# Attention inside a hybrid block on one core: single-bank score tiles in a ring of three, values left with channels on partitions, row sums inverted on a small tile, q and k stored in halves

## The chip, the cores and the metric

The kernel runs on one core of a Trainium2 chip, as one program. The time is device microseconds from the first to the last instruction of the program, and smaller is better. The names of the engines are those of the profile: PE is TensorE (PEld its weight loads), ACT ScalarE, DVE VectorE, POOL GpSimd, SP SyncE.

## The reference, cut to what matters

Four layers follow each other on x of shape 16 x 1024 x 256: windowed attention, a mixture of experts, full attention, and the mixture of experts again, each on a layer norm of x and added to x. The change touches the third.

```python
def _L0_attn_b_ref(x, w_qkv, w_o):
    b, s, hid = x.shape                      # 16, 1024, 256
    heads, d = 16, hid // 16                 # 16 heads of 16 channels
    qkv = x @ w_qkv.T * hid ** (-0.5)
    qkv = qkv.reshape(b, s, 3, heads, d)
    q, k, v = (jnp.transpose(qkv[:, :, i], (0, 2, 1, 3)) for i in range(3))
    scores = jnp.einsum('bhqd,bhkd->bhqk', q, k) * d ** (-0.5)
    attn = jax.nn.softmax(scores, axis=-1) * (s / np.sqrt(s - 1.0))
    out = jnp.einsum('bhqk,bhkd->bhqd', attn, v) * s ** (-0.5)
    out = jnp.transpose(out, (0, 2, 1, 3)).reshape(b, s, hid)
    return out @ w_o.T * hid ** (-0.5)
...
x = x + _L0_attn_b_ref(_layernorm(x, axis=-1), L0_attn_b_w_qkv, L0_attn_b_w_o)
```

## The kernel before, in words

`projection_stage` (names with cp_) makes q, k and v for 32 groups of 512 tokens and stores them to DRAM. q and k are stored twice, as a rounded part ("hi") and the rest ("lo"), so that products can be taken in the fast float32r form.

`attention_stage` (names with at_) works on 128 **pairs**: two heads of one batch, 8 pairs to a batch, 16 batches. The loop over pairs is unrolled. Every engine has its own written list of instructions, and semaphores join them.

For one pair, the scores are computed twice.

- **Scores by query** (`scores_by_query`, L1830): 16 steps (8 tiles of 128 queries by 2 halves of the keys), each two matmuls of 128x512, one for each head, into one of the two buffers psM (two banks each). DVE takes the maximum over each (`maximum`, L1773, 128x1024 elements). They run 5 query tiles more than one pair ahead (`LEAD`). After 16 of them `mx` (L1777) joins the halves, PE turns it (`max_rows`, L1836), ACT negates it (`take_max`, L1721), POOL splits it into hi and lo (`split_max`), and SP writes the two as rows 48 and 49 of the queries' tile (`load_max`, L1618 and L1619). The matmul then subtracts the maximum by itself.
- **Scores by key** (`scores_by_key`, L1846): 32 tiles of 128 keys by 512 queries. psE has three banks. The tiles are taken in 21 groups of 2, 1, 2, 1, ... tiles (`GROUPS`): the twos use banks 0 and 1, the ones bank 2. A group's matmul waits for the exponential of the group two before (`p_ready`), and ACT takes the exponential of a whole group in one instruction (`exps`, L1729), of 1024 or 512 elements a partition.
- **Values** (`values`, L1857): for each of 8 key tiles, 8 matmuls of 256 queries, in four column groups of the array, gather probabilities times (v, 1) into the one bank psO, with 16 channels and the row sum on partitions. A pair's last two key tiles are done in the next pair.

The result of a pair: ACT copies psO to OT (`take_values`, L1734), PE turns it back into psO with four transposes (`turn_values`, L1867), DVE takes the reciprocal of the sums and multiplies (`normalise`, L1784 and L1788) into O. Four pairs later PE turns pieces of O (`turn_out`, L1873), ACT copies them (`take_out`, L1739), POOL splits them (`split_out`, L1683 and L1686), and `project_out` (L90 with at_w) makes one unit of 128 tokens of the output in bank 2. ACT scales it (`scale_y`, L1744), POOL adds x (`add_x`, L1693), and SP stores it (L1630) and loads the next x (L1622).

The order on PE is written out by hand in `pair`: each `key(g)`, `query(m, g)` and `values(...)` stands at a fixed place. PE, DVE and ACT take their lists strictly in turn, and so does SP, which per pair waits for the pair before to be through with its tiles, issues 9 loads of q, k and v for the pair three ahead, then 4 for the maxima, one store and one load.

Of the kernel before, what the change touches and what calls it, by code (L numbers as in the profile page):

```python
# [1275 lines left out]
def projection_stage(nc, T, stage, x, wT, qk, v):  # L1276
# [5 lines left out]
    G = 512  # L1282
# [3 lines left out]
    qkb = qk.rearrange("r (b h) d n -> b r (h d) n", h=H)  # L1286
    vb = v.rearrange("b p s h k w -> s b p h k w")
    with ExitStack() as ctx:
# [34 lines left out]
        def _(sp):  # L1323
# [156 lines left out]
def attention_stage(nc, T, stage, x, qk, v, woT, out):  # L1480
# [10 lines left out]
    NG = 21  # L1491
    OUT_SCALE = S / float(S - 1) ** 0.5 * S ** -0.5 * D ** -0.5
    xb = x.rearrange("(b p q c) d -> b c q p d", q=4, c=2, p=128)
    ob = out.rearrange("(b q c p) d -> b c q p d", q=4, c=2, p=128)
    qkp = qk.rearrange("r (u x) d n -> u x r d n", x=2)
    vp = v.rearrange("b p s (u x) k w -> u b p s (x k w)", x=2)
    with ExitStack() as ctx:
# [11 lines left out]
        rden = sb("rden", [128, 2, KC], F32)  # L1509
        O = sb("o", [128, KC, D], F32)  # L1510
# [23 lines left out]
        oT_ready, t_done, o_ready, rden_ready = sem("oT_ready"), sem("t_done"), sem("o_ready"), sem("rden_ready")  # L1534
        xo_done, xo_taken, xo_hi_ready, xo_lo_ready = sem("xo_done"), sem("xo_taken"), sem("xo_hi_ready"), sem("xo_lo_ready")
# [7 lines left out]
        GROUPS = [(3 * g // 2, 2) if g % 2 == 0 else ((3 * g + 1) // 2, 1) for g in range(NG)]  # L1543
        HOLDS = [next(g for g in range(NG) if GROUPS[g][0] + GROUPS[g][1] > u) for u in range(4 * KC)]
        LEAD = 5
        OUT_AT, MAX_AT, VALUES_AT, NORM_AT = 1, 11, 3, 3
# [39 lines left out]
        def load_queries(eng, pp, j):  # L1586

            for a in range(2):
                r = 64 * a
                eng.dma_start(Q[j][r:r + 32, :].bitcast(F32), row(qkp, pp)[a, 0:2]).then_inc(qk_loaded[j], 16)  # L1590
                eng.dma_start(Q[j][r + 32:r + 48, :].bitcast(F32), row(qkp, pp)[a, 0]).then_inc(qk_loaded[j], 16)

        def load_keys(eng, pp, j):

            for a in range(2):
# [3 lines left out]
                eng.dma_start(K[j][r:r + 16, :].bitcast(F32), row(qkp, pp)[a, 2]).then_inc(qk_loaded[j], 16)  # L1599
                eng.dma_start(K[j][r + 16:r + 48, :].bitcast(F32), row(qkp, pp)[a, 2:4]).then_inc(qk_loaded[j], 16)  # L1600
# [6 lines left out]
        def _(sp):  # L1607
# [13 lines left out]
            def load_x(b, n):  # L1621
                sp.dma_start(X[n][:], row(xb, b)[n // 4, n % 4]).then_inc(x_loaded[n], 16)  # L1622

            def store_out(u, b, n):
# [29 lines left out]
            batches(pair)
            store_out(NP - 9, B - 2, PB - 1)
            for n in range(PB):
                store_out(PB * B - PB + n, B - 1, n)
            for n in range(PB):
                sp.wait_ge(y_stored[n], 16 * B)

        @block.gpsimd
        def _(pool):
# [343 lines left out]
```

## Time and profile before

| | before |
|---|---|
| median of 3 runs | 5755.92 us (5751.49 to 5757.47) |
| the profiled execution's own time | 5750.62 us |
| its span | 5748.9 us |
| granted TensorE clock, mean | 0.976 |
| PE, PEld busy | 94%, 64% |
| DVE, ACT, POOL busy | 78%, 62%, 26% |

The attention stage is slices 15 to 33 of the page's 40 (about 2005 to 4799 us), nearly half of the kernel. PE's busy time is modelled: matmuls overlap in the array, so PE can stand at 100% and still have waited. What PE waited for is seen at its weight loads (PEld), since each matmul's load carries the wait. In the list of DMA issues the columns are KB each and us from issue to landing. In the timeline a row is a run of like instructions: start, duration, engine, line, count, and in brackets the idle time ahead and who ended it.

### The profile page before, as it was taken

The page shows a single profiled execution, that of the slowest core. Times are in us where ns is not written, and L with a number is a line of the kernel's source. Part 1 is how long each engine was busy: PE and PEld are TensorE (multiplying, and loading weights), DVE is VectorE, ACT ScalarE, POOL GpSimd, SP SyncE. Part 2 cuts the span into 40 slices and gives each one's busy share as a digit, 9 for nine tenths or more (in the row PEclk, how much of TensorE's full clock was granted, in tenths as well). Part 3 has the DMA queues.
Part 4 walks back from the last instruction along what each step waited for, and adds up shares of the span by engine and source line. Part 5 has one row for each costly group of instructions (what it writes and reads, how often), then busy time and mean ns, then how long its engine had stood idle before and what let it go on. Part 6 is the DMA issues. An engine that isn't in the chain of part 4 may idle for free. (4 is left out here: it accounts for less than half of the span.)

```text
span 5748.9 us, 131254 instructions
## 1 busy us (share of the span) xinstructions
PE 5428.0 (94%) x50092; PEld 3660.4 (64%) x50092; DVE 4498.2 (78%) x7377; ACT 3566.0 (62%) x5406; POOL 1473.5 (26%) x1948
## 2 busy tenths in 40 slices
PE   7999668999989889999999999999999997799999
PEld 6777457999978734444444444444444444699998
DVE  7888695555557689999999999999999996755554
ACT  5777562333325458888888888888888886433332
POOL 4655453333310000111111111111111114533332
PEclk9999889999999989999999999999999998999999
DMA  2222482222229811121112111111211113222221
GB/s 74 78 84 78 137 259 77 88 93 93 89 96 333 310 56 49 58 60 57 57 59 60 57 56 60 59 57 56 60 58 57 57 54 104 75 89 93 95 86 49
DMA packets 317697, 512.58 MB, mean 89 GB/s; under 512 B 36442, under 2 KB 221156, under 8 KB 311152
## 3 DMA queue, kind: packets, MB, share of 16 engines
q1 hardware_dynamic: 291912, 441.44, 24.2%
q0 software_dynamic: 24576, 64.56, 3.5%
q8 instruction: 271, 4.44, 0.3%
q10 hardware_dynamic: 808, 1.07, 0.1%
q14 instruction: 130, 1.06, 0.1%
HBM read 338.59 MB, written 185.60 MB: 91 GB/s over the span
## 5 line engine op out<-in xcount | busy, mean ns | idle before, releaser
L1773 DVE TENSOR_REDUCE at_best<-at_psM 128x2 f32<-128x1024 f32 x2048 | 2430.7, 1221 | 227.5 <-PE at_psM L1830 214.3
L1729 ACT ACTIVATE at_p<-at_psE 128x1024 f32<-128x1024 f32 (+1 forms) x2688 | 2077.1, 824 | 529.5 <-PE at_psE L1846 515.7
L1846 PE MATMUL at_psE<-at_q,at_k 50*128 50x512 f32 x4096 | 1174.0, 436 | 7.5 <-ACT at_p L1729 6.3
L1830 PE MATMUL at_psM<-at_k,at_q 48*128 48x512 f32 x4096 | 1093.6, 458 | 37.5 <-DMA at_k<-scratch_qk 27.4
L1857 PE MATMUL at_psO<-at_p,at_v 128*17 128x256 f32 x16384 | 1109.9, 383 | 0.1
L1122 ACT ACTIVATE e_h_hi<-e_psH 128x512 fp32r<-128x512 f32 x512 | 306.7, 599 | 916.0 <-PE e_psH L90 864.4
L1846 PEld LDWEIGHTS at_psE<-at_q,at_k 50*128 50x128 f32 x4096 | 548.7, 185 | 462.4 <-issue 223.6
L1196 DVE SCALAR_TENSOR_TENSOR e_h_lo<-e_psH,e_h_hi 128x512 fp32r<-128x512 f32 x512 | 353.9, 691 | 595.9 <-ACT e_h_hi L1122 505.8
L1857 PEld LDWEIGHTS at_psO<-at_p,at_v 128*17 128x17 f32 x16384 | 364.1, 96 | 542.7 <-issue 345.4
L1830 PEld LDWEIGHTS at_psM<-at_k,at_q 48*128 48x128 f32 x4096 | 471.3, 185 | 312.2 <-DVE at_best L1773 147.2
L90 PE MATMUL e_psE<-e_w_hi,e_h_hi 128*128 128x256 f32 x2048 | 583.1, 285 | 0.0
L90 PE MATMUL e_psE<-e_w_hi,e_h_lo 128*128 128x256 f32 x2048 | 579.6, 283 | 0.0
L90 PE MATMUL e_psE<-e_w_lo,e_h_hi 128*128 128x256 f32 x2048 | 579.3, 283 | 0.0
L90 PE MATMUL e_psH<-e_xhi,e_w_hi 128*128 128x512 f32 x1024 | 406.8, 397 | 4.7 <-DVE e_xlo L1163 4.7
L90 PE MATMUL e_psH<-e_xlo,e_w_hi 128*128 128x512 f32 x1024 | 406.1, 397 | 0.0
L90 PEld LDWEIGHTS e_psE<-e_w_hi,e_h_hi 128*128 128x128 f32 x2048 | 391.3, 191 | 21.6 <-issue 1.2
L90 PEld LDWEIGHTS e_psE<-e_w_lo,e_h_hi 128*128 128x128 f32 x2048 | 391.4, 191 | 17.3
L90 PE MATMUL e_psH<-e_xhi,e_w_lo 128*128 128x512 f32 x1024 | 400.0, 391 | 0.0
L90 PEld LDWEIGHTS e_psE<-e_w_hi,e_h_lo 128*128 128x128 f32 x2048 | 391.1, 191 | 0.0
L1672 POOL CAST at_nm_hi<-at_nm 16x128 fp32r<-16x128 f32 x128 | 36.0, 282 | 1258.3 <-ACT at_nm L1721 1258.3
L1693 POOL TENSOR_TENSOR at_y<-at_y,at_x 128x256 f32<-128x256 f32 x120 | 87.5, 729 | 1029.9 <-ACT at_y L1744 1029.9
L258 POOL COPY a_pt<-a_pc 32x512 f32<-32x512 f32 x384 | 236.1, 615 | 114.7 <-PE a_psO L541 32.7
(213 smaller groups left out, 8456.5 us busy)
## 6 DMA issues: line engine op xcount, KB each, us to landing
e_w_raw<-in_w SPq DMA_DIRECT2D x64, 1024.0 KB
scratch_qk<-cp_qkh SPq DMA_DIRECT2D x64, 512.0 KB
scratch_qk<-cp_qkl SPq DMA_DIRECT2D x64, 512.0 KB
at_q<-scratch_qk SPq DMA_DIRECT2D x256, 128.0 KB
at_k<-scratch_qk SPq DMA_DIRECT2D x252, 128.0 KB
scratch_v<-cp_va SPq DMA_DIRECT2D x32, 544.0 KB
at_v<-scratch_v SPq DMA_DIRECT2D x126, 136.0 KB, 10.0
a_x<-in_x SPq DMA_DIRECT2D x32, 512.0 KB
```

The lines of the kernel that those rows point to most:

```text
L90: last = nc.tensor.matmul(out, a, b, start=start and n == 0, stop=stop and n == len(products) - 1, **kw)
L258: nc.gpsimd.tensor_copy(PT[b][r, :, r], PC[b][r, :, :]).then_inc(pt_ready, 1)
L1122: nc.scalar.activation(h_hi[f % 2][:], psH[f % 2][:, 0:G], ACT.Relu).then_inc(h_hi_ready, 1)
L1196: nc.vector.scalar_tensor_tensor(out=h_lo[f % 2][:], in0=psH[f % 2][:, 0:G], scalar=0.0, in1=h_hi[f % 2][:].bitcast(F32), op0=ALU.max, op1 ...
L1672: nc.gpsimd.tensor_copy(nm_hi[s][:], nm[s][:]).then_inc(nm_hi_ready, 1)
L1693: nc.gpsimd.tensor_tensor(Y[n][:], Y[n][:], X[n][:], ALU.add).then_inc(y_ready, 1)
L1729: nc.scalar.activation(P[:, u:u + n, :], src, ACT.Exp, scale=HD ** -0.5).then_inc(p_ready, 1)
L1773: nc.vector.reduce_max(best[j % 2][:, h, :, qt], psM[h][:], AX_X).then_inc(m_taken, 1)
L1830: last = nc.tensor.matmul(psM[h][:, a, :], Q[j][r, 128 * qt:128 * qt + 128], K[j][r, 512 * h:512 * h + 512], start=True, stop=True)
L1846: last = nc.tensor.matmul(psE[:, u - u0 if n == 2 else 2, :], K[j][r, 128 * kc:128 * kc + 128], Q[j][r, 512 * half:512 * half + 512], star ...
L1857: last = nc.tensor.matmul(psO[32 * q:32 * q + HD + 1, 256 * a:256 * a + 256], V[j][:, kc // 4, a, kc % 4, :], P[:, 4 * kc + 2 * (q // 2) + ...
```

## The change

1. **Score ring.** `GROUPS` goes. Each of the 32 tiles is a unit of its own with its own exponential of 512 elements; psE is a ring of three banks in which the tiles, `max_rows` (before tile 14) and `project_out` (before tile 19) take turns (`IN_TURN`, `bank`, `wait_for_bank`). A tile's matmul waits for the user of its bank three turns before. PE's list in `pair` is written anew, and the values of a pair lag more: key tiles 3 to 7 are done in the next pair.
2. **Values stay with channels on partitions.** `turn_values`, `normalise`, `turn_out` and `take_out` go. SP stores OT to DRAM (`store_values`) and moves the sums, SBUF to SBUF, onto a tile of 128x16 (`sums`). DVE inverts that (`invert`, after its maximum 11 of 16). SP stores it (`store_inverses`), and four pairs later loads values and inverses back, the latter repeated over 16 channels (`load_unit`). POOL multiplies (`split_out`). The end of the stage has tiles of its own (`divide_end`).
3. **q and k in halves.** The DRAM tensor is split by half of the sequence, so `projection_stage` stores contiguous blocks, and `load_queries` and `load_keys` issue 12 loads of 16 rows by 2 by 512 in place of 8, four of which had 32 rows.
4. **Order elsewhere.** SP's and POOL's lists are rearranged; tokens of x and of the output are taken in plain tiles of 128 strided by 8.

```diff
-    NG = 21
+    NU, BANKS = 4 * KC, 3
-        OUT_AT, MAX_AT, VALUES_AT, NORM_AT = 1, 11, 3, 3
+        OUT_AT, MAX_AT, VALUES_AT, INVERT_AT = 19, 14, 14, 11
+        IN_TURN = [user for u in range(NU) for user in (["out"] if u == OUT_AT else ["max"] if u == MAX_AT else []) + [u]]
+        def bank(pp, user):
+            return psE[:, turn_at_bank(pp, user) % BANKS, :]
...
+            def store_values(p):
+                sp.wait_ge(oT_ready, p + 1)
+                sp.dma_start(ot[p].rearrange("a r c -> r a c"), OT[:].rearrange("r (a c) -> r a c", a=2)).then_inc(oT_stored, 16)
...
+                    sp.dma_start(sums[p % 2][:], OT[HD:128:32, :].rearrange("q (w e) -> q w e", e=16)).then_inc(sums_moved, 16)
+            def load_unit(u, slot, b, k, m, needed):
...
+                sp.dma_start(raw[slot][:], rows[b, k, m][:, 0:HD, :]).then_inc(unit_loaded[slot], 16)
+                sp.dma_start(den[slot][:], inverse_rows[b, k, m].unsqueeze(1).broadcast_to([8, HD, 256])).then_inc(unit_loaded[slot], 16)
...
             def split_out(u, slot, k, m, b):
-                pool.wait_ge(xo_taken, u + 1)
+                pool.wait_ge(unit_loaded[slot], 32 * (u // 2 + 1))
+                after(pool, xo_lo_ready, u - 1)
+                nc.gpsimd.tensor_tensor(oT[slot][:], raw[slot][:], den[slot][:], ALU.mult).then_inc(ofT_ready, 1)
+                pool.wait_ge(ofT_ready, u + 1)
                 after(pool, wo_done, PB * (b - 1) + 2 * m + 2)
...
+            def exps(pp, u):
+                act.wait_ge(e_done, NU * pp + u + 1)
+                if u % 4 == 0:
+                    after(act, pv_done, KC * (pp - 1) + u // 4 + 1)
+                nc.scalar.activation(P[:, u, :], bank(pp, u), ACT.Exp, scale=HD ** -0.5).then_inc(p_ready, 1)
             def take_values(p):
                 act.wait_ge(pv_done, KC * p + KC)
-                after(act, t_done, p)
+                after(act, oT_stored, 16 * p)
+                after(act, sums_moved, 16 * p)
...
+            def invert(p):
+                dve.wait_ge(sums_moved, 16 * (p + 1))
+                nc.vector.reciprocal(sums[p % 2][:], sums[p % 2][:]).then_inc(rden_ready, 1)
...
+                last_values(3), keys(0), query(0, 1), keys(1), query(1, 2), keys(2), last_values(4, (0,))
+                last_values(4, (1,)), keys(3, 5), query(2, 5), keys(5), last_values(5, (0,))
+                keys(6), query(3, 7), keys(7), last_values(5, (1,)), query(4, 8), keys(8, 11), last_values(6)
+                query(5, 11), keys(11, 13), query(6, 13), keys(13), last_values(7)
+                next_max_rows(), query(7, 14), keys(14, 16), query(8, 16), keys(16), values(pp, pb % 4, 0)
+                keys(17, 19), query(9, 19), output(), keys(19), query(10, 20), keys(20), query(11, 21)
+                keys(21), values(pp, pb % 4, 1, (0,)), keys(22, 24), values(pp, pb % 4, 1, (1,)), query(12, 24), keys(24), query(13, 25)
+                keys(25, 27), values(pp, pb % 4, 2, (0,)), keys(27), query(14, 28), keys(28), values(pp, pb % 4, 2, (1,))
+                keys(29), query(15, 30), keys(30, 32)
```

In the lists at_psE<-at_q,at_k is a score tile by key, at_psM<-at_k,at_q one by query, at_psO<-at_p,at_v the values. PE before, from the output unit of a steady pair to the turned values:

```order
L90 MATMUL at_psE<-at_w_hi,at_oT_lo 128x256
L1830 MATMUL at_psM<-at_k,at_q 128x512 x2
L1846 MATMUL at_psE<-at_q,at_k 128x512 x2
L1857 MATMUL at_psO<-at_p,at_v 17x256 x8
L1830 MATMUL at_psM<-at_k,at_q 128x512 x4
L1846 MATMUL at_psE<-at_q,at_k 128x512 x3
L1857 MATMUL at_psO<-at_p,at_v 17x256 x8
L1846 MATMUL at_psE<-at_q,at_k 128x512
L1830 MATMUL at_psM<-at_k,at_q 128x512 x2
L1846 MATMUL at_psE<-at_q,at_k 128x512 x2
L1867 MATMUL at_psO<-ident,at_oT 128x128 x4
```

PE in the change, from query step 3 of a steady pair to key tile 13:

```order
L1900 MATMUL at_psM<-at_k,at_q 128x512 x2
L1927 MATMUL at_psE<-at_q,at_k 128x512
L1937 MATMUL at_psO<-at_p,at_v 17x256 x4
L1900 MATMUL at_psM<-at_k,at_q 128x512 x2
L1927 MATMUL at_psE<-at_q,at_k 128x512 x3
L1937 MATMUL at_psO<-at_p,at_v 17x256 x8
L1900 MATMUL at_psM<-at_k,at_q 128x512 x2
L1927 MATMUL at_psE<-at_q,at_k 128x512 x2
L1900 MATMUL at_psM<-at_k,at_q 128x512 x2
L1927 MATMUL at_psE<-at_q,at_k 128x512
```

Key tiles now come one by one, three in a row at most, and some value blocks are halved; the transposes of the values are gone from the list.

SP before, from the last loads of k to the end of a steady pair:

```order
L1599 DMA at_k<-scratch_qk 16x1024
L1600 DMA at_k<-scratch_qk 32x1x1024
L1604 DMA at_v<-scratch_v 128x2x136
L1618 DMA at_q<-at_nm_hi 1x8x128
L1619 DMA at_q<-at_nm_lo 1x8x128
L1618 DMA at_q<-at_nm_hi 1x8x128
L1619 DMA at_q<-at_nm_lo 1x8x128
L1630 DMA out_x<-at_y 128x256
L1622 DMA at_x<-scratch_x 128x256
```

SP in the change, from the loads of q and k of a steady pair to its end:

```order
L1608 DMA at_q<-scratch_qk 16x2x512 x6
L1617 DMA at_k<-scratch_qk 16x2x512 x6
L1621 DMA at_v<-scratch_v 128x2x136
L1655 DMA scratch_ot<-at_oT 128x2x256
L1659 DMA at_sums<-at_oT 128x1x16
L1635 DMA at_q<-at_nm_hi 1x8x128
L1636 DMA at_q<-at_nm_lo 1x8x128
L1635 DMA at_q<-at_nm_hi 1x8x128
L1636 DMA at_q<-at_nm_lo 1x8x128
L1665 DMA scratch_rd<-at_sums 4x32x16
L1647 DMA out_x<-at_y 128x256
L1639 DMA at_x<-scratch_x 128x256
```

The value and sum transfers stand ahead of the four for the maxima, the inverses behind them; with the two loads of a unit, which stand in front, SP issues 24 transfers a pair, 15 before.

## Rows read from the trace of the kernel before

**Rows 1.** Windows, steady stretch (stretch, length, busy us by engine, PEclk, DMA share, GB/s).

```profile
3500.00:4000.00 500.00, 500.00 (x4809) 246.15 (x4809) 459.31 (x445) 404.34 (x586) 58.98 (x116) 1.00 0.19 58
```

**Rows 2.** Groups by line and form, 3000 to 4500 us.

```profile
L1773 DVE TENSOR_REDUCE at_best<-at_psM 128x2 f32<-128x1024 f32 x1126 | 1337.7, 1221 | 116.2 <-PE at_psM L1830 108.4
L1729 ACT ACTIVATE at_p<-at_psE 128x1024 f32<-128x1024 f32 x774 | 792.5, 1024 | 96.4 <-PE at_psE L1846 89.2
...
L1729 ACT ACTIVATE at_p<-at_psE 128x512 f32<-128x512 f32 x703 | 424.2, 603 | 188.9 <-PE at_psE L1846 188.9
...
L1686 POOL TENSOR_TENSOR at_oT_lo<-at_ofT,at_oT_hi 128x256 fp32r<-128x256 f32 x70 | 51.2, 731 | 12.6 <-POOL at_oT_hi L1683 12.6
...
L1777 DVE TENSOR_TENSOR at_mx<-at_best 128x16 f32<-128x16 f32 x71 | 12.4, 175 | 2.4
```

**Rows 3.** Waits, 3000 to 4500 us (waiting engine <- releaser: total us, times, longest).

```profile
ACT at_p L1729 <- PE at_psE L1846: 278.0, 632, 0.8
...
DVE at_best L1773 <- PE at_psM L1830: 108.4, 351, 0.5
PEld at_psE L1846 <- ACT at_p L1729: 102.5, 351, 0.4
POOL at_oT_hi L1683 <- PE at_psE L90: 80.6, 9, 9.0
PEld at_psM L1830 <- DVE at_best L1773: 67.7, 212, 0.4
```

**Rows 4.** Timeline of the stage's start, PE clock still at half.

```profile
2024.13 1.22 PE L1830 MATMUL at_psM<-at_k,at_q 48*128 48x512 f32 x4 [27.43 <-DMA at_k<-scratch_qk]
2024.97 18.19 DVE L1773 TENSOR_REDUCE at_best<-at_psM 128x2 f32<-128x1024 f32 x16 [15.31 <-PE at_psM L1830]
2026.25 0.80 PE L1830 MATMUL at_psM<-at_k,at_q 48*128 48x512 f32 x2 [0.90 <-DVE at_best L1773]
...
2051.39 0.64 SPq L1619 DMA_DIRECT2D at_q<-at_nm_lo  x1
...
2054.26 0.66 PE L1846 MATMUL at_psE<-at_q,at_k 50*128 50x512 f32 x2
```

**Rows 5.** Timeline of one steady pair, DVE and ACT.

```profile
4001.25 0.60 ACT L1734 ACTIVATE at_oT<-at_psO 128x512 f32<-128x512 f32 x1
4001.73 3.15 ACT L1729 ACTIVATE at_p<-at_psE 128x512 f32<-128x512 f32 x4
...
4002.88 0.25 DVE L1784 RECIPROCAL at_rden<-at_psO 128x16 f32<-128x16 f32 x1
4003.16 0.42 DVE L1788 TENSOR_TENSOR at_o<-at_psO,at_rden 128x256 f32<-128x256 f32 x1
4003.50 2.35 DVE L1773 TENSOR_REDUCE at_best<-at_psM 128x2 f32<-128x1024 f32 x2
```

**Rows 6.** Timeline of three places in a steady pair, PE, ACT and DVE.

```profile
3500.01 1.06 PE L1857 MATMUL at_psO<-at_p,at_v 128*17 128x256 f32 x16
...
3501.00 0.49 PE L1846 MATMUL at_psE<-at_q,at_k 50*128 50x512 f32 x1
...
3514.16 0.50 PE L1846 MATMUL at_psE<-at_q,at_k 50*128 50x512 f32 x1
...
3514.69 1.51 ACT L1729 ACTIVATE at_p<-at_psE 128x512 f32<-128x512 f32 x2 [0.38 <-PE at_psE L1846]
...
3520.22 0.50 PE L1830 MATMUL at_psM<-at_k,at_q 48*128 48x512 f32 x2
...
3520.76 3.56 DVE L1773 TENSOR_REDUCE at_best<-at_psM 128x2 f32<-128x1024 f32 x3 [0.44 <-PE at_psM L1830]
```

**Rows 7.** SP's issue of one 16-row load; DMA issues of one pair; a window of it.

```profile
3534.16 0.40 SPq L1591 DMA_DIRECT2D at_q<-scratch_qk  x1
...
at_v<-scratch_v SPq DMA_DIRECT2D x1, 136.0 KB, 10.1
...
out_x<-at_y SPq DMA_DIRECT2D x1, 128.0 KB, 4.2
...
3542.00:3543.00 1.00, 1.00 (x15) 0.53 (x15) 0.91 (x1) 0.68 (x2) 0.00 (x0) 1.00 0.14 52
```

**Rows 8.** Timeline of the last two pairs, of which DVE has next to nothing, and of the end.

```profile
4747.78 0.60 ACT L1734 ACTIVATE at_oT<-at_psO 128x512 f32<-128x512 f32 x1
...
4768.49 0.60 ACT L1734 ACTIVATE at_oT<-at_psO 128x512 f32<-128x512 f32 x1
...
4786.26 0.60 ACT L1734 ACTIVATE at_oT<-at_psO 128x512 f32<-128x512 f32 x1 [1.18 <-PE at_psO L1857]
...
4789.39 1.42 DVE L1812 TENSOR_TENSOR at_oT_lo<-at_psM,at_oT_hi 128x256 fp32r<-128x256 f32 x4 [1.07 <-ACT at_oT_hi L1766]
```

**Rows 9.** Windows, projection stage.

```profile
1800.00:1820.00 20.00, 19.92 (x117) 16.46 (x115) 14.39 (x40) 9.67 (x16) 0.00 (x0) 1.00 0.97 334
```

More of the change, by code:

```diff
@@ L1477, in _, with attention_stage @@
             groups(pe, NG, group)
[L1480 removed]
+def attention_stage(nc, T, stage, x, qk, v, ot, rd, woT, out):
     N, D = x.shape
@@ L1654, in _ @@
             batches(pair)
+            store_values(NP - 1)
+            sp.wait_ge(oT_stored, 16 * NP)
+            for m in range(4):
+                span = slice(256 * m, 256 * m + 256)
+                sp.dma_start(end_den[:, span], rows[B - 1, 1, m][:, HD:HD + 1, :].broadcast_to([8, HD, 256])).then_inc(end_loaded[m], 16)
+                sp.dma_start(end_raw[:, span], rows[B - 1, 1, m][:, 0:HD, :]).then_inc(end_loaded[m], 16)
             store_out(NP - 9, B - 2, PB - 1)
@@ L1659, in _ @@
                 sp.wait_ge(y_stored[n], 16 * B)
+            for s in range(2):
+                sp.wait_ge(rden_stored[s], 16 * (NP // 2 - s))
         @block.gpsimd
@@ L1697, in pair @@
             def pair(pp, pb, b):
+                if there(pp + 1):
+                    split_max(pp + 1, (pb + 1) % 4, turn_of(pp, pb, b, -1) + 1 if not first(pp) else 0)
                 if has_out(pp):
@@ L1700, in pair @@
                     add_x(u, ub, n)
-                if there(pp + 1):
-                    split_max(pp + 1, (pb + 1) % 4, turn_of(pp, pb, b, -1) + 1 if not first(pp) else 0)
                 if has_turned(pp):
@@ L1832, in scores_by_query, with wait_for_bank @@
                 last.then_inc(m_done, 1)
-            def max_rows(p, j):
+            def wait_for_bank(pp, user):
+                n = turn_at_bank(pp, user) - BANKS
+                while n >= 0:
+                    pp, before = n // len(IN_TURN), IN_TURN[n % len(IN_TURN)]
+                    if before == "out" and has_out(pp):
+                        return pe.wait_ge(y_scaled, pp - 8)
+                    if before == "max" and there(pp + 1):
+                        return pe.wait_ge(nm_ready, pp + 2)
+                    if before != "out" and before != "max":
+                        return pe.wait_ge(p_ready, NU * pp + before + 1)
+                    n = n - 1
@@ L1900, in query, with keys @@
                         scores_by_query(mp, mj, turn_of(pp, pb, b, 1 if m // 2 < KC - LEAD else 2), qt, m % 2,
[L1901 to L1911 removed]
+                                        u % 2)
+                def keys(u, end=0):
+                    for each in range(u, max(u + 1, end)):
+                        scores_by_key(pp, pb % 4, turn_of(pp, pb, b, 0), each)
                 def last_values(kc, heads=(0, 1)):
@@ L1934, in pair @@
-                output(), query(0, -1), key(0), last_values(6)
-                query(1, 0), query(2, 0), key(1), key(2), last_values(7)
-                key(3), query(3, 3), key(4)
-                if not first(pp):
-                    turn_values(pp - 1)
-                key(5), query(4, 5), query(5, 5), key(6), values(pp, pb % 4, 0)
-                key(7), query(6, 7), key(8), values(pp, pb % 4, 1)
-                key(9), query(7, 9), key(10), query(8, 10), turns(), values(pp, pb % 4, 2, (0,))
@@ L1942, in pair @@
-                query(9, 10), key(11), key(12), values(pp, pb % 4, 2, (1,))
-                values(pp, pb % 4, 3, (0,)), query(10, 12), key(13), query(11, 13), key(14), values(pp, pb % 4, 3, (1,))
-                values(pp, pb % 4, 4, (0,)), key(15), query(12, 15), key(16), values(pp, pb % 4, 4, (1,))
-                key(17), query(13, 17), query(14, 17), key(18), key(19), values(pp, pb % 4, 5)
-                key(20), query(15, 20)
+                        project_out(ub, n, bank(pp, "out"))
```

218 lines of the change are left out of this document (108 added, 110 removed).

## Prediction

> **What bounds the kernel now.** I read the windows of the steady stretch first, then the groups, the waits, and the timeline of single pairs. A pair takes 1500 us / (1126 / 16) = 21.31 us [rows 2], and 128 pairs are nearly the whole stage. In the windows PE is busy all the time, DVE 92%, ACT 81% [rows 1]; none of these is the floor. DVE's floor is in the start of the stage, where nothing but maxima run: 16 in 18.19 us, so (18.19 - 1.22) / 15 = 1.131 us each, 18.1 us a pair [rows 4]. The reciprocal and the product cost it 4003.50 - 4002.88 = 0.62 us [rows 5], `mx` 0.18 [rows 2]: 18.9 us, so DVE stands 2.4 us of each pair. ACT loses more: it waits for score tiles 278.0 us in this stretch, 3.9 us a pair [rows 3]. PE waits for ACT 102.5 us and for DVE 67.7 us at these two tiles alone, 1.5 and 1.0 us a pair [rows 3].
>
> So the three wait for one another. The telling rows are those of the last pair but one: from one copy of the values to the next it takes 4768.49 - 4747.78 = 20.71 us [rows 8], though DVE has almost nothing left to do there. The bound is the loop of PE and ACT through psE. The reason is in its geometry: a group of two tiles can only be refilled when its own exponential is through, and only the one-tile exponential covers that. From the row at 3514.69, 1.51 - 1.02 = 0.49 us is the step of a 512-element exponential with work waiting, and PE's key tile at 3514.16 was 0.53 us ahead of it [rows 6]; 0.53 + 0.05 against 0.49 and the second tile's 0.1 leaves ACT idle before each large group, 0.38 us in that row.
>
> **The change part by part.**
>
> *Ring.* ACT's floor: 32 exponentials at 0.48 (the step from 4001.25 to 4001.73 [rows 5]) are 15.4 us, with the copies of values, maxima and output about 16.3 us. A bank now has two other exponentials, 0.96 us, to be refilled in, against 0.05 + 0.53 = 0.58 us needed, so PE may be 0.4 us late before ACT stands. PE gains freedom, but ACT runs closer to it.
>
> *PE.* Gone are six transposes (0.9 us by the timeline's gaps, an estimate from the 0.5 to 1.0 us pieces of [rows 6]), and the waits for OT and for the group ahead. Added are entries into value blocks: a block of 16 instructions takes 3501.00 - 3500.01 = 0.99 us [rows 6], two halves a little more together. I take PE's work as 17.5 us, below DVE's.
>
> *DVE.* Product and half the cost of the reciprocal go: 18.1 + 0.18 + 0.25 (the reciprocal's own 0.25 [rows 5], its input now in SBUF) = **18.55 us, the new floor**. What comes on top is how late PE brings a query step. A step may start 2026.25 - 2024.97 = 1.28 us after the start of the maximum two before it [rows 4], and the next maximum can start 3520.76 - 3520.22 = 0.54 us after the step [rows 6]; 1.28 + 0.54 = 1.82 against 2 x 1.131 leaves PE 0.44 us of slack. I followed PE's new list with 0.11 us a score tile, 0.99 or 0.56 us a value block or half, 0.9 us for the output unit and these lags. Three places lose time. Tiles 8 to 10 wait for exponentials 5 to 7, the block of key tile 6 follows, and query step 5 comes 0.5 us late. Step 10 behind the output unit is 0.1 late. At the pair's end tiles 29 to 31 and another block stand between steps 15 and 0, 0.4 us. The sum is 18.55 + 1.0 = 19.6 us; I take **19.7 us**, since entries into blocks were left out. The ends are 18.55 us (no gap) and 18.55 + 2.4 = 20.95 us (DVE's gaps stay). The saving is 128 x (21.3 - 19.7) = **205 us**, between 350 and 45.
>
> *SP.* It issues 24 transfers a pair instead of 15. At the 0.64 us of the row at 2051.39 [rows 4] that is 15.4 us of 19.7, with its waits in between. The loads of q and k start at the pair's head, and are through (12 x (0.40 [rows 7] + 0.05) = 5.4 us) before the values of the pair before are done (about 8.5 us in, by the walk above). Hidden, if the pair is no shorter than 16 us; otherwise the issue itself is the floor.
>
> *The trip of the sums.* ACT copies the values after its tile 13, about 9.5 us in. SP issues the store and then the small transfer (by 10.7 us); the nearest small transfer, the last row of the maxima, was issued at 2051.39 and its reader ran at 2054.26, so 2.9 us at most [rows 4]. The sums are there at 13.6 us; DVE wants them after maximum 11, 12 x 1.14 + 1 = 15 us in. Hidden by 1.4 us. The range of landings is 2.9 to 10.1 us, the latter of the values' load [rows 7]; I take the small one, because the 10 us are those of a transfer queued behind slow loads. What queues behind it: every later maximum on DVE, and with it PE's query steps.
>
> *Loads of q and k.* While the 32-row loads ran, the DMA share was 0.14 and 52 GB/s [rows 7], some two engines of 16. The new form has 16 rows. This shortens queueing in every pair, which costs nothing there, and the wait at the stage's start, 27.43 us [rows 4]: I take 6 us off, of 0 to 12. The Trainium skill (DMA: Bandwidth & Descriptors, Rules for kernel authors) says that the outermost dimension of the patterns sets how many engines a transfer gets, and a source of 2 x 16 x 1024 would get two; the trace agrees with its 0.14, and by that rule the gain would be the upper end.
>
> *POOL.* It gets one product more, at the 0.73 us of the row of L1686 [rows 2], in 15 us of slack. But it takes its list in turn, and `split_out` of a batch's last unit waits for that span's output unit of the batch before. It did so 9 times for 9.0 us [rows 3]. The unit now stands 12 us into the next pair instead of at its head, and `split_max` is queued behind. From there: 12.4 + 1.1 for the split + 0.8 for `split_max` + 2.0 for SP + 2.9 to land = 19.2 us, against 19.7 when the next pair's first tile needs it. I take 0.5 us for 15 batches, **8 us**, between 0 and 30.
>
> *End of stage.* The last pair has three more value blocks behind its exponentials (3 us, some of it given back by a first pair that has them not). From the copy at 4786.26 to the first difference at 4789.39 it took 3.1 us [rows 8]; now two transfers to and from DRAM at 4.2 us each [rows 7] and some 1.5 us of DVE and ACT lie there: **9 us** more, between 5 and 12.
>
> *Projection stage.* 32 stores become contiguous. PE is busy 19.92 of 20 us [rows 9], so nothing, between -5 and +3.
>
> Against the profiled execution's own time: 5750.6 - 205 - 6 + 8 + 9 = 5557 us. The median of the runs lies 5.3 us above that execution, so 5562; I say **5560 us**.
>
> **The rivals.**
>
> 1. *The gaps stay.* PE serves two rings from one list, and the ring by key wants service every 0.48 us. DVE's gaps of 2.4 us stay and 0.3 us or more is all that is saved: 20.6 to 21 us a pair, 5650 to 5715 us. For it: PE's slack of 0.44 us is half a value block. Against it: the 20.71 us of a pair without DVE [rows 8] belong to the geometry that goes.
> 2. *The sums come late, and it is slower.* Place: the wait ahead of `invert`. If the transfer lands later than 15 - 10.7 = 4.3 us after its issue, all of the excess stops DVE in every pair. From 4.3 + 1.6 = 5.9 us it eats the gain. At the 10.1 us of the values' load [rows 7] a pair takes 19.7 + 5.8 = 25.5 us, and the kernel 5560 + 128 x 5.8 = 6300 us; at 7 us, 5905. For it: 64-byte pieces, and a queue with 24 transfers. Against it: the slow loads ahead of it go.
> 3. *A fixed cost for each exponential.* ACT has 11 exponentials more a pair. At the whole 603 ns of a single one [rows 2] 32 are 19.3 us, with the copies 20.5 us a pair, 5665 us, already a smaller gain. The Trainium skill (ScalarE: Activation LUTs, Rules for kernel authors) gives about 0.3 us an instruction and 0.83 ns an element, which would be 32 x 0.72 = 23 us, and a kernel some 300 us slower. The trace disagrees: the step is 0.48 to 0.49 us [rows 5, 6].
> 4. *Nothing moves*, because a chain over pairs (maxima, POOL, SP) takes the place: 21.3 us.
>
> **How the numbers follow.** The forecast has 0.72: pairs of 18.9 to 20.5 us, 5450 to 5665 us. Rival 1 has 0.15, all of it faster. Rival 2 has 0.07, rival 3 has 0.02 and rival 4 has 0.04, most of it within the bound. About 0.2%, 12 us, is what a measurement of this kernel can tell from no change. Faster: 0.72 + 0.15 + 0.01 = 0.88; same 0.03; slower 0.07 + 0.02 = 0.09. The range reaches down to 5450 and up to 5680 us, which takes in the lower part of rival 1 and leaves out 0.05 below and 0.15 above.
>
> **What the profile will show.** Maxima every 19.5 to 20 us by sixteen, with DVE at 93 to 95%. ACT's wait for score tiles from 3.9 to about 2 us a pair, its exponentials in long unbroken runs. No wait of DVE on the sums; their landing under 4 us. q and k landed 6 us after the first issue. A longer wait of PE for ACT at single tiles would show rival 1; a wait "DMA at_sums" on DVE, rival 2; ACT near 100% busy, rival 3. I am wrong in the reason if the pair gets shorter while ACT's wait for PE stays.

## The result, and the profile after

| | before | changed |
|---|---|---|
| median | 5756.69 us (5751.49 to 5758.22, 4 runs) | 5680.16 us (5677.24 to 5697.62, 4 runs) |
| ratio, 95% interval | | 0.9875 [0.9854, 0.9896] |
| profiled execution, span | 5750.62, 5748.9 | 5697.62, 5695.9 |
| DVE, ACT, PE busy | 78%, 62%, 94% | 78%, 64%, 94% |

The change is faster, by 76.5 us (1.3%); the forecast was 196 us, and 5680.2 lies just above its range. The direction came true, the size did not.

First the steady stretch again. Windows of the changed kernel, with the columns of [rows 1, 7, 9]:

```profile
3500.00:4000.00 500.00, 497.52 (x4817) 228.03 (x4817) 458.17 (x436) 429.64 (x846) 80.61 (x147) 1.00 0.30 87
1800.00:1820.00 20.00, 19.88 (x118) 16.27 (x116) 14.29 (x38) 9.84 (x18) 0.00 (x0) 1.00 0.96 336
```

DVE is as busy as in [rows 1], 92%, not the 93 to 95% that I named. The second row answers to [rows 9]: the projection stage did not move. Groups and waits of 3000 to 4500 us, as in [rows 2, 3]:

```profile
L1839 DVE TENSOR_REDUCE at_best<-at_psM 128x2 f32<-128x1024 f32 x1160 | 1360.2, 1220 | 124.1 <-PE at_psM L1900 117.9
L1801 ACT ACTIVATE at_p<-at_psE 128x512 f32<-128x512 f32 x2320 | 1214.0, 598 | 207.2 <-PE at_psE L1927 178.0
```

```profile
PEld at_psE L1927 <- ACT at_p L1801: 196.7, 508, 0.4
...
ACT at_p L1801 <- PE at_psE L1927: 178.0, 437, 0.7
POOL at_oT_hi L1757 <- PE at_psE L90: 169.6, 9, 18.8
...
DVE at_best L1839 <- PE at_psM L1900: 117.9, 290, 0.6
```

1160 / 16 = 72.5 pairs in 1500 us are 20.69 us each, 0.6 less than before. From copy to copy of the values the trace gives 20.70 us, the same to 0.07 us in the whole steady stretch. ACT's wait for score tiles fell from 3.9 to 178.0 / 72.5 = 2.5 us a pair, as the ring was meant to do. DVE's did not fall: 117.9 / 72.5 = 1.6 us against 1.5. The timeline of one pair shows where it stands:

```profile
4001.16 1.06 PE L1937 MATMUL at_psO<-at_p,at_v 128*17 128x256 f32 x16
...
4002.14 0.50 PE L1900 MATMUL at_psM<-at_k,at_q 48*128 48x512 f32 x2
...
4002.69 1.23 DVE L1839 TENSOR_REDUCE at_best<-at_psM 128x2 f32<-128x1024 f32 x1 [0.53 <-PE at_psM L1900]
...
4002.96 0.40 PE L1927 MATMUL at_psE<-at_q,at_k 50*128 50x512 f32 x1
...
4003.28 1.06 PE L1937 MATMUL at_psO<-at_p,at_v 128*17 128x256 f32 x16
...
4007.75 1.23 DVE L1839 TENSOR_REDUCE at_best<-at_psM 128x2 f32<-128x1024 f32 x1 [0.22 <-PE at_psM L1900]
...
4009.31 2.36 DVE L1839 TENSOR_REDUCE at_best<-at_psM 128x2 f32<-128x1024 f32 x2 [0.34 <-PE at_psM L1900]
...
4011.59 0.24 DVE L1849 RECIPROCAL at_sums<-at_sums 128x16 f32<-128x16 f32 x1
...
4016.92 5.93 DVE L1839 TENSOR_REDUCE at_best<-at_psM 128x2 f32<-128x1024 f32 x5 [0.53 <-PE at_psM L1900]
...
4023.41 1.23 DVE L1839 TENSOR_REDUCE at_best<-at_psM 128x2 f32<-128x1024 f32 x1 [0.56 <-PE at_psM L1900]
```

DVE stands ahead of step 5 (4002.69), behind the output unit (4009.31) and at the pair's end (4016.92, with the next pair's step 5 again at 4023.41). These are the three places of the prediction, but with larger gaps, and a small fourth stands ahead of step 9 (4007.75). And look at PE's rows: a value block takes 4002.14 - 4001.16 = 0.98 us, as read before, but it starts 4003.28 - 4002.96 = 0.32 us behind the last tile, where tiles follow each other in about 0.12. That is 0.2 us at each entry into a block, which stands in no row by itself.

The ends of the stage. Its start, as in [rows 4], then its end, as in [rows 8]:

```profile
2033.00 1.22 PE L1900 MATMUL at_psM<-at_k,at_q 48*128 48x512 f32 x4 [16.47 <-DMA at_k<-scratch_qk]
```

```profile
4706.51 0.62 ACT L1807 ACTIVATE at_oT<-at_psO 128x512 f32<-128x512 f32 x1
...
4707.72 0.57 SPq L1659 DMA_DIRECT2D at_sums<-at_oT  x1
...
4709.65 0.25 DVE L1849 RECIPROCAL at_sums<-at_sums 128x16 f32<-128x16 f32 x1 [18.80 <-DMA at_sums<-at_oT]
...
4720.47 0.60 ACT L1807 ACTIVATE at_oT<-at_psO 128x512 f32<-128x512 f32 x1 [3.48 <-PE at_psO L1937]
...
4727.22 1.75 DVE L1855 RECIPROCAL at_end_den<-at_end_den 128x256 f32<-128x256 f32 x1 [17.32 <-DMA at_end_raw<-scratch_ot]
...
4732.16 0.42 DVE L1882 TENSOR_TENSOR at_oT_lo<-at_end_raw,at_oT_hi 128x256 fp32r<-128x256 f32 x1
```

PE waited 16.47 us for k, against 27.43: 11.0 us less. At the end 4732.16 - 4720.47 = 11.7 us lie between the last copy of values and the first difference, against 3.1 before, 8.6 more. Landings, as in [rows 7]:

```profile
at_q<-scratch_qk SPq DMA_DIRECT2D x768, 64.0 KB, 2.4
...
at_v<-scratch_v SPq DMA_DIRECT2D x126, 136.0 KB, 2.6
```

The values' load lands in 2.6 us in place of 10.1, without a change of its own.

**The sum of the stage** against the trace before: first copy of values 8.2 us later behind the first matmul (the blocks that lag, and a clock that stayed at half for some 15 us more, an estimate from windows of 20 us; the two are not separated), the 127 intervals to the last copy 4720.47 - 2100.1 = 2620.4 us against 2703.2, 82.8 less, and 12.4 more from there to the next stage. With the start's 11.0 that is 73 us less. In this execution the stages ahead, whose code is the same but for the stores of q and k, took 19.8 us longer. That fits its place 17 us above the median: in the traces of the other runs those stages take from 0.7 us less to 17 us more than before, without a pattern by kernel.

### The profile page after: what moved, and what is told of

Its sections match the earlier page's. It is cut to its first block and busy times, and to the rows that moved or that the text cites. A ratio compares the mean times of both kernels' runs of the same rounds, so it can differ in the third digit from the quotient of the medians.

```text
span 5695.9 us, 132881 instructions
## 1 busy us (share of the span) xinstructions
PE 5349.4 (94%) x49324; PEld 3536.3 (62%) x49324; DVE 4424.5 (78%) x7256; ACT 3631.7 (64%) x6690; POOL 1564.1 (27%) x2072
## 5 line engine op out<-in xcount | busy, mean ns | idle before, releaser
L1839 DVE TENSOR_REDUCE at_best<-at_psM 128x2 f32<-128x1024 f32 x2048 | 2400.2, 1220 | 227.3 <-PE at_psM L1900 216.6
L1801 ACT ACTIVATE at_p<-at_psE 128x512 f32<-128x512 f32 x4096 | 2144.8, 598 | 378.2 <-PE at_psE L1927 327.4
L1927 PE MATMUL at_psE<-at_q,at_k 50*128 50x512 f32 x4096 | 1253.4, 433 | 4.0 <-ACT at_p L1801 3.8
L1937 PE MATMUL at_psO<-at_p,at_v 128*17 128x256 f32 x16384 | 1160.6, 384 | 0.0
L1900 PE MATMUL at_psM<-at_k,at_q 48*128 48x512 f32 x4096 | 1068.0, 454 | 37.9 <-DMA at_k<-scratch_qk 16.5
L1927 PEld LDWEIGHTS at_psE<-at_q,at_k 50*128 50x128 f32 x4096 | 582.6, 186 | 459.5 <-ACT at_p L1801 361.9
L1937 PEld LDWEIGHTS at_psO<-at_p,at_v 128*17 128x17 f32 x16384 | 338.4, 96 | 589.6 <-ACT at_p L1801 251.7
L1900 PEld LDWEIGHTS at_psM<-at_k,at_q 48*128 48x128 f32 x4096 | 443.5, 187 | 342.5 <-issue 157.5
L1074 POOL DMA_INDIRECT out_x<-e_y,e_index x124 | 127.9, 1032 | 363.9 <-DVE e_y L1176 334.1
```

The lines of the kernel that those rows point to most:

```text
L1074: nc.gpsimd.indirect_dma_start(x, bass.IndirectOffsetOnAxis(ap=index[q][:, t:t + 1], axis=0), Y[s][:, t, :], None, bounds_check=N - 1, oob ...
L1801: nc.scalar.activation(P[:, u, :], bank(pp, u), ACT.Exp, scale=HD ** -0.5).then_inc(p_ready, 1)
L1839: nc.vector.reduce_max(best[j % 2][:, h, :, qt], psM[h][:], AX_X).then_inc(m_taken, 1)
L1900: last = nc.tensor.matmul(psM[h][:, a, :], Q[j][r, 128 * qt:128 * qt + 128], K[j][r, 512 * h:512 * h + 512], start=True, stop=True)
L1927: nc.tensor.matmul(bank(pp, u), K[j][r, 128 * kc:128 * kc + 128], Q[j][r, 512 * half:512 * half + 512], start=True, stop=True).then_inc(e_ ...
L1937: last = nc.tensor.matmul(psO[32 * q:32 * q + HD + 1, 256 * a:256 * a + 256], V[j][:, kc // 4, a, kc % 4, :], P[:, 4 * kc + 2 * (q // 2) + ...
```

## The experiments

Two theories for the 20.70 us. **P**: PE's own list is far longer than my 17.5 us, so that it is the floor, and DVE's and ACT's waits are what it leaves. **D**: the three engines wait for one another, as before, and PE has room. Each kernel is the changed one with the edit shown, and "pair" is the interval between copies of values in the steady stretch. Where nothing else is said, a kernel was executed once, and its time is good to some 10 us; the pair is sharper.

**1. Half of the maxima.** The maximum is taken over 256 of the 512 keys of each half, so the value subtracted is another one.

```diff
-                nc.vector.reduce_max(best[j % 2][:, h, :, qt], psM[h][:], AX_X)
+                nc.vector.reduce_max(best[j % 2][:, h, :, qt], psM[h][:, :, 0:256], AX_X)
```

> The changed kernel, but DVE takes each maximum over 256 of the 512 keys of a bank, so half of the candidates are left out; PE and ACT do all that they did. A maximum shrinks from 1.13 to about 0.60 us, DVE's work in a pair from 18.5 to about 10 us. A steady pair of the changed kernel takes 20.70 us. Theory P (PE's list is the bound: score tiles, value blocks and the entries and exits between them add up to about 20 us): 20.1 to 20.5 us a pair. Theory D (DVE is the floor with 18.55 us and PE's lateness comes on top, as predicted): the slack grows, the gaps go, and a pair falls below 19 us.

Measured: 5616.8 us, pair 20.22. DVE was relieved of some 8 us a pair (its busy time in the 500 us window is 271 in place of 458), and 0.48 us came of it. DVE alone is not the floor; whether DVE and ACT together hold PE up is left for 4.

**2. Half of the values.** PE's value matmuls take 128 of 256 queries; the other columns of psO hold 1.0.

```diff
-  psO[32 * q:32 * q + HD + 1, 256 * a:256 * a + 256], ... P[..., 256 * (q % 2):256 * (q % 2) + 256]
+  psO[32 * q:32 * q + HD + 1, 256 * a:256 * a + 128], ... P[..., 256 * (q % 2):256 * (q % 2) + 128]
```

> The changed kernel, but each value matmul takes 128 of its 256 queries, so half of the values is left out; all instructions, waits, entries and exits stay. PE saves about 8 x 0.43 = 3.4 us a pair. Theory P: the pair falls from 20.70 to DVE's floor with small gaps, 18.6 to 19.3 us. Theory D: the saved time is on an engine that waits anyway, except at the gaps of DVE behind a block; 19.5 to 20 us. A theory L in which the latency of the loop PE to ACT and back sets the pair: 20.3 us or more.

Measured: 5618.0 us, pair 19.13, once the clock was up. PE's work is what counts: 1.57 us less. Windows, an early and a steady stretch:

```profile
2460.00:2480.00 20.00, 20.00 (x148) 9.81 (x150) 13.86 (x14) 12.95 (x26) 0.73 (x2) 0.50 0.25 77
2600.00:3000.00 400.00, 391.00 (x4166) 204.86 (x4168) 390.63 (x378) 371.39 (x733) 67.91 (x125) 1.00 0.33 93
```

Steady, DVE is busy 98% of the time and is now the bound. The early row is a surprise, told below; without it the run would have been some 130 us shorter (127 intervals at 19.13 us are 2430 us, and they took 2560).

**3. Half of the exponentials.** Each covers 256 of 512 queries; the rest of P is 1.0.

```diff
-  nc.scalar.activation(P[:, u, :], bank(pp, u), ACT.Exp, ...)
+  nc.scalar.activation(P[:, u, 0:256], bank(pp, u)[:, 0:256], ACT.Exp, ...)
```

> The changed kernel, but ACT takes each exponential over 256 of a tile's 512 queries; the other half of the probabilities stays at 1.0, set once by DVE at the stage's start (some 20 us there). An exponential shrinks from 0.48 to about 0.27 us. With all maxima halved instead, a pair took 20.22 us against 20.70. Theory P (PE's own list is the bound): 20.4 to 20.7 us a pair. A theory A, in which ACT's step of 0.48 us in the ring of three sets when PE's next tile may start: below 19.8 us.

Measured: 5687.9 us, pair 20.70. ACT's 32 steps by themselves don't bound the pair, and rival 3 is out with them.

**4. PE alone.** The edits of 1 and 3 together.

> The changed kernel with both relieved: maxima over half of the keys, exponentials over half of the queries (the rest of the probabilities is 1.0). PE's list is whole. Neither DVE nor ACT should hold PE up, so the pair is PE's list by itself. Theory P: 19.9 to 20.2 us, hardly below the 20.22 us with halved maxima. If waits of PE for the two still made up the pair: 18.5 us or less, what the prediction's 17.5 us of work on PE would allow.

Measured: 5616.3 us, pair 20.19. With both other engines at 54 to 57% (row below), a pair takes as long as with the maxima alone halved. So 20.2 us is PE's own list, in this order, and D is out.

```profile
3500.00:4000.00 500.00, 500.00 (x4936) 232.61 (x4936) 271.39 (x447) 283.82 (x868) 80.04 (x146) 1.00 0.31 88
```

**5. Fewer and more entries.** The changed order enters value blocks 11 times a pair, five whole and six halves. First three splits were joined, in the whole kernel and with PE alone:

```diff
-  last_values(5, (0,)) ... last_values(5, (1,)) ... values(pp, pb % 4, 1, (0,)) ... values(pp, pb % 4, 1, (1,)) ...
+  ... last_values(5) ... values(pp, pb % 4, 1) ...
```

> The changed kernel, but the halved value blocks (key tiles 5, 1 and 2) are made whole, at the place of their second half: 8 blocks a pair in place of 11. If PE's time were only its sum, three entries and exits less (0.33 us each) would give 20.70 - 1.0 = 19.7 us. If PE must also come back to DVE within 0.44 us and to ACT within 0.4 us, whole blocks in these places starve both: 21 to 21.6 us a pair. The second is what theory P with DVE's slack expects.

Measured: 5838.3 us, pair 21.93, far worse; PE's waits for ACT at the key tiles grew from 196.7 to 237.8 us in the 1500 us, and DVE's for PE from 117.9 to 190.4.

> The kernel with whole value blocks (8 a pair in place of 11), and with halved maxima and halved exponentials as in the run beside it. The two differ by three entries into a block and three exits, with nothing else holding PE. Theory P puts 0.3 to 0.4 us on each: 1.0 us less than the run beside it, 19.0 to 19.2 us. If a switch between score tiles and values cost only what the prediction took (0.13 us, the exit alone): 0.4 us less.

Measured: 5610.3 us, pair 20.20. A miss: nothing gained. The timeline says why:

```profile
3501.26 0.89 PE L1928 MATMUL at_psE<-at_q,at_k 50*128 50x512 f32 x2
...
3501.66 0.18 PEld L1928 LDWEIGHTS at_psE<-at_q,at_k 50*128 50x128 f32 x1 [0.44 <-ACT at_p L1801]
```

Joined blocks put five key tiles between two value blocks, with only query steps among them, and a ring of three banks lets three through; the next waits for an exponential (the weight load stood 0.44 us here). So I went the other way, with PE alone and three more blocks split, at places where no row of tiles gets longer:

```diff
-  keys(8, 11), last_values(6)
+  keys(8, 10), last_values(6, (0,)), keys(10), last_values(6, (1,))
...
-  keys(13), last_values(7)
+  last_values(7, (0,)), keys(13), last_values(7, (1,))
...
-  keys(16), values(pp, pb % 4, 0)
+  values(pp, pb % 4, 0, (0,)), keys(16), values(pp, pb % 4, 0, (1,))
```

> Against pe_alone (5616.3 us, steady pair 20.19 us) three more blocks of values are split, so PE enters a block of values 14 times a pair in place of 11, and no stretch of score tiles gets longer. If each entry and leaving costs PE about 0.33 us, as read from the trace (0.2 before the first value matmul, 0.12 behind the last), the pair takes 21.0 to 21.3 us and the run about 5735 us. If entries cost nothing, or are hidden by the wait for banks, the pair stays at 20.2 us and the run at 5616 us.

Measured: 5729.0 us, pair 21.12. Three entries cost 0.93 us, **0.31 us each** for the way in and out, as read from the timeline.

**6. The old ring, without the transposes.** Groups of two and one tile and PE's order of before, with the new way of the values.

```diff
-        OUT_AT, MAX_AT, VALUES_AT, INVERT_AT = 19, 14, 14, 11
+        OUT_AT, MAX_AT, VALUES_AT, INVERT_AT = 1, 11, 3, 11
+        GROUPS = [(3 * g // 2, 2) if g % 2 == 0 else ((3 * g + 1) // 2, 1) for g in range(NG)]
...
+                output(), query(0, -1), key(0), last_values(6)
...
```

> The changed kernel with the score tiles in groups of two and one as before, each group one exponential, and PE's order of before less the six transposes; the values' new way through DRAM, the inverses and the loads of q and k in halves stay. Before has 21.33 us a pair, the change 20.70. If the ring brings the gain (the prediction's reason), this is 21.0 to 21.3 us. If the transposes and their waits bring it, 20.4 to 20.8 us, and the ring nothing.

Measured: 5837.4 us. Seven pairs in eight take 21.10 us, the eighth 27.3 to 28.7. So from 21.33, the transposes and DVE's product are worth 0.23 us, and ring and order together 0.40 us. The two were not taken apart; the order has a price of its own, since PE enters value blocks 11 times a pair in place of 9. The eighth pair is a wait by itself:

```profile
3297.95 0.72 POOL L1755 TENSOR_TENSOR at_ofT<-at_raw,at_den 128x256 f32<-128x256 f32 x1 [9.32 <-DMA at_den<-scratch_rd]
...
3300.35 0.29 PEld L90 LDWEIGHTS at_psE<-at_w_hi,at_oT_hi 128*128 128x128 f32 x1 [5.20 <-issue]
```

A batch's first unit stands at the pair's head there. Its inverses land late, and PE waits up to 5.6 us for POOL's split, while the changed kernel has the unit behind tile 18 and loses nothing. This is not the chain that I had put at 8 us under *POOL*; that one shows in 8.

**7. The halves alone.** The kernel before, with q and k stored and loaded in halves.

```diff
-                eng.dma_start(Q[j][r:r + 32, :].bitcast(F32), row(qkp, pp)[a, 0:2])
-                eng.dma_start(Q[j][r + 32:r + 48, :].bitcast(F32), row(qkp, pp)[a, 0])
+                for n, kind in enumerate((0, 1, 0)):
+                    eng.dma_start(Q[j][r + 16 * n:r + 16 * n + 16, :].bitcast(F32), row(qkp, pp)[a, kind])
```

> The kernel before with nothing but q and k stored and loaded in halves (12 loads of 16 rows in place of 8). Steady pairs: no difference from 21.33 us, since the loads have two pairs of time. Start of the stage: PE's first wait 27.4 us becomes 16 to 17 us, so the kernel is 9 to 12 us faster in all. If the shorter wait at the changed kernel's start comes from elsewhere, no difference.

Measured: 5741.7 us, below every execution of the kernel before (5748.1 to 5759.7). The pair is unmoved (21.33) and PE's wait at the start 10.7 us shorter: the halves act there only.

**8. Other orders for PE.** The same instructions; only `pair`'s list on PE and the four constants differ. If PE's 20.2 us are the floor, the changed order still leaves 0.5 us.

> The changed kernel, same instructions, with PE's list in another order: 11 visits to value blocks as before, but steps spread more evenly, the transpose at key tile 8 in the shadow of other work and the projection at key tile 25; the maxima lead by six query tiles in place of five. If PE's 20.2 us of work is the floor and the rest (0.5 us a pair, DVE's gaps ahead of steps 0, 5, 9 and 10) is bad placing, the pair goes to 20.2 to 20.5 us and the run to 5620 to 5660. If the placing is as good as it can be, it stays at 20.7 or gets worse (5680 to 5720).

> As order_a, with the lead left at five: two steps at the head of the pair, projection at tile 16 and transpose at tile 18. Placing theory: 20.3 to 20.5 us a pair (5630 to 5660). Floor theory: 20.7 or more (5680 or more).

> As order_b with another order: six of the eight value blocks at the head whole, projection at tile 15, transpose at 17. Placing theory: 20.3 to 20.5 us a pair (5630 to 5660). Floor theory: 20.7 or more (5680 or more).

> PE's list with the projection at key tile 18, the transpose at 20, and the values taken at tile 16, three blocks split more than order_c has and fewer maxima late in a row. If order_b and order_c are already at the floor that PE's list sets, 20.5 us a pair (5656); if placing has more to give, 20.3.

> The transpose at tile 21 and the projection at 27, values taken at tile 19. Floor theory: 20.5 us (5656) or more; placing theory: 20.2 to 20.4. It could be worse for one reason of its own: the transposed maxima have less time before the next pair's first score tile.

Measured: a 6094.7 us (pairs 22.2 to 25.3, and one longer in each batch), b 5667.0 (20.50), c 5656.4 (20.50), d 5676.1 (20.65), e 5779.7. In e seven pairs in eight take 20.55 us, as in b and c; at each batch's end from the second on, one takes 26.2 to 30.9 us. These 14 pairs cost 112 of the 123 us between e and c. They are the chain that I had priced at 8 us under *POOL*:

```profile
3263.32 0.40 POOL L1757 CAST at_oT_hi<-at_ofT 128x256 fp32r<-128x256 f32 x1 [18.70 <-PE at_psE L90]
...
3264.56 0.28 POOL L1741 CAST at_nm_hi<-at_nm 16x128 fp32r<-16x128 f32 x1
...
3267.51 0.64 SPq L1636 DMA_DIRECT2D at_q<-at_nm_lo  x1
...
3269.32 0.79 PE L1927 MATMUL at_psE<-at_q,at_k 50*128 50x512 f32 x2 [3.00 <-DMA at_q<-at_nm_lo]
...
3272.00:3276.00 4.00, 4.00 (x25) 1.59 (x19) 1.23 (x1) 1.58 (x3) 1.18 (x3) 0.50 0.64 189
```

POOL waits for the output unit, which e has before tile 27 instead of 19, and splits the maxima only then; PE stands 3.00 us for their rows. Behind that wait PE's granted clock is 0.50 until about 3284 us (last row), which goes with the rest of that pair's 10.3 us. In the changed kernel the last of these rows is issued at 3247.19 us and PE's first tile starts at 3250.37. With e's 1.8 us from issue to start that leaves 1.4 us to spare.

In a the transpose stands right behind the step whose maxima it turns:

```profile
4015.32 0.27 PE L1919 MATMUL at_psE<-ident,at_mx 128*16 128x128 f32 x1 [1.62 <-DVE at_mx L1843]
```

That is one cause of its 1.5 us and more. At its batch ends PE waits for the maxima's rows as in e (2.66 us in one of them; these pairs take up to 31.5 us), and its mean granted clock over 3000 to 4500 us is 0.92, against 1.00 in c; how the 1.5 and 3 us between its other pairs divide was not traced. The best, c, again in five executions, beside four of the changed kernel:

```diff
-        OUT_AT, MAX_AT, VALUES_AT, INVERT_AT = 19, 14, 14, 11
+        OUT_AT, MAX_AT, VALUES_AT, INVERT_AT = 15, 17, 13, 11
...
+                last_values(3), keys(0, 2), query(0, 2), keys(2), last_values(4, (0,)), keys(3)
+                query(1, 4), keys(4), last_values(4, (1,)), keys(5), query(2, 6), keys(6)
+                last_values(5), keys(7), query(3, 8), keys(8), query(4, 9), keys(9)
+                last_values(6), keys(10), query(5, 11), keys(11, 13), last_values(7), keys(13)
+                query(6, 14), query(7, 14), keys(14), output(), keys(15, 17), query(8, 17)
+                next_max_rows(), values(pp, pb % 4, 0, (0,)), keys(17), query(9, 18), keys(18, 20), values(pp, pb % 4, 0, (1,))
+                keys(20), query(10, 21), keys(21), values(pp, pb % 4, 1, (0,)), keys(22), query(11, 23)
+                keys(23, 25), values(pp, pb % 4, 1, (1,)), keys(25), query(12, 26), keys(26, 28), query(13, 28)
+                keys(28), values(pp, pb % 4, 2), keys(29, 31), query(14, 31), keys(31), query(15, 32)
```

> Repeat of order_c with rounds, beside the changed kernel: 5650 to 5662 us, 15 to 30 us under it, as in the one look (5656.4; steady pair 20.50 against 20.70, 0.20 by 125 pairs = 25 us).

> The changed kernel again, unaltered, beside order_c5: 5675 to 5685 us, as its fastest three runs of four were.

Measured: c 5656.16 us (5655.2 to 5664.4), ratio to before 0.9834 [0.9821, 0.9848]; the changed kernel 5681.74, 0.9872 [0.9857, 0.9887]. The intervals don't meet: c beats both kernels, by 25.6 us over the change. DVE in c's first execution, in one pair of the timeline:

```profile
4002.74 3.49 DVE L1839 TENSOR_REDUCE at_best<-at_psM 128x2 f32<-128x1024 f32 x3 [0.42 <-PE at_psM L1900]
...
4006.74 7.21 DVE L1839 TENSOR_REDUCE at_best<-at_psM 128x2 f32<-128x1024 f32 x6 [0.31 <-PE at_psM L1900]
...
4016.80 6.01 DVE L1839 TENSOR_REDUCE at_best<-at_psM 128x2 f32<-128x1024 f32 x5 [0.26 <-PE at_psM L1900]
4023.25 1.23 DVE L1839 TENSOR_REDUCE at_best<-at_psM 128x2 f32<-128x1024 f32 x1 [0.43 <-PE at_psM L1900]
```

The same kind of gap, but smaller: 76.1 us of waits for PE in 1500 us, against 117.9.

## Why the prediction was right and wrong

- **The step that failed is PE's work, "I take PE's work as 17.5 us, below DVE's".** With the other engines relieved PE's list takes 20.2 us, 2.7 us more, and above DVE's floor of 18.55. I had named the entries into blocks and given them the difference between 19.6 and 19.7. They cost 0.31 us each, 11 of them 3.4 us, of which the 0.12 us of the way out was in my 0.99 us a block. The 17.5 us was a guess over the sum of my own walk and had no row behind it. In the trace of experiment 4 the 20.2 us can be added up from matmul start to matmul start (3000 to 4500 us, a pair): 6.8 us in 52 steps from tile to tile, 3.7 in 11 steps from a tile into a block (0.33 each), 3.4 in 11 steps out of a block (0.31 each), 4.9 inside the blocks, 1.2 for the output unit with its ways in and out, and 0.2 behind the transpose. The kernel before has the same step into a block, 0.325 us in the median, and enters blocks 9 times a pair. The price could have been read beforehand, and two of the 11 entries are the change's own.
- **The walk over PE's list found the right places and too small gaps.** It carried the same missing 0.2 us at each entry, so every step that stands behind a block came later than I had it. DVE's gaps beyond its own work add up to 20.70 - 18.55 = 2.15 us, against 1.0 to 1.15 forecast. The saving of a pair was 0.63 us, not 1.6.
- **Rival 1 came true in its number** (20.70, within its 20.6 to 21 us), but not by its reason alone: DVE's gaps stayed because PE has no time to spare, not mainly because two rings ask at once. That second cause is the 0.5 us between 20.2 and 20.7, of which another order gave 0.2 back. Its times were added up wrongly, too: by the sum of the forecast 20.6 to 21 us a pair are 5675 to 5726 us, not 5650 to 5715, so that a range up to 5680 held next to nothing of it.
- **"The bound is the loop of PE and ACT through psE"** was half right. Ring and order gave 0.40 us and ACT's wait fell to 2.5 us; but halving the exponentials gave nothing, so ACT's round trip no longer binds. The transposes and the product, counted in PE's and DVE's floors, gave 0.23. The pair of 20.71 us on which I had built this lacked more than DVE's work: PE had only some 5 of its 32 query matmuls left in it. The pair at the same place of the changed kernel has none, and from copy to copy (4687.42 to 4706.51) it takes 19.1 us. So the loop did give about 1.6 us there. In a steady pair PE's list stands right behind it.
- **Start of stage:** 11.0 us against 6 of 0 to 12. The upper end, which the rule of the Trainium skill (DMA: Bandwidth & Descriptors, Rules for kernel authors) gave, was right, and 7 confirms it by itself at 10.7.
- **POOL's batch boundary:** 8 us forecast, none there. POOL's own wait grew as expected, to 18.8 us at the longest, but no pair is longer than its neighbours. My own sum, 19.2 us against 19.7, had left half a microsecond to spare, and I took it for a loss. The chain itself is real: 1.4 us are to spare in the changed kernel, and where the output unit comes eight tiles later (e) it costs 6 to 10 us a batch.
- **End of stage:** 12.4 us more against 9 of 5 to 12, just outside; 8.6 of it between last copy and first difference, the other 3.8 behind that, where DVE's four reciprocals of 1.75 us follow each other; I had "some 1.5 us of DVE and ACT". The first pair's share, 8.2 us, I had nearly set to nothing ("some of it given back"); the last two intervals gave some 4 back.
- **Projection and sums:** nothing, as said. DVE does not wait for the sums in the steady stretch. At the stage's end, where it has nothing else to do, it starts on them 4709.65 - 4707.72 = 1.9 us after the issue. Rivals 2 and 3 did not occur; 3's 603 ns is 598 ns of duration at a step of about half a microsecond.

## What to carry to other kernels

Before taking an engine as free, price its list by starts, not by durations: the difference from one row's start to the next across a change of kind (here score tile to value block, 0.32 us in place of 0.12) is a cost that no group shows. Where three engines stay near 90%, take work from each in turn; whichever answers is the bound. And once the bound is a written order, its places are worth as much as its contents: the same instructions in another order gave 26 us, a third of what the change gave, while two other orders cost 98 and 413. Before moving an entry of such a list, look at who waits for it once in eight turns and not in every one: without the 112 us at its batch boundaries, the order that cost 98 us would have been faster than the change.

## What had not been expected of the hardware

- **The clock stayed low with half the values.** PE's granted clock at the start of the stage is at half, 1.2 GHz, after the wait for q and k. In the changed kernel it rose between 2080 and 2100 us and is 1.00 from there (before, it was 0.81 already over 2060 to 2080). With half the values it was still 0.50 at 2480 us (the first row shown in experiment 2), with pairs of 28.04 us in place of 19.13, though PE shows as busy for all of those 20 us, and was 1.00 from 2500 us.
- **A wait of 3.0 us went with a loss of 10.** In order e PE stood for 3.00 us at a batch's end. The granted clock had been 1.00 over 3260 to 3266 us; behind the wait it was 0.50 from 3269 to 3284 us, though PE was busy, and the pair took 10.3 us more.
- **Splitting a block of matmuls costs 0.31 us** where the form on both sides differs, though all the data are ready.
- **Three banks pass three tiles.** A fourth with no value block between waits up to 0.44 us, even with exponentials half as long; merging blocks to save entries gives the gain back there.
